# A macaron layer on one core: the first norm spread between the decode's picks, and the first feed-forward in a ring of three PSUM banks

## The reference

```python
x = x + 0.5 * ffn(layernorm(x))      # w = lut[idx]; silu(x Wg) * (x Wu), then Wd; inner size 688
x = x + mamba2(layernorm(x))         # 64 heads of 64, state 128, one group, chunk scan, gated RMS norm
x = x + 0.5 * ffn(layernorm(x))
```

## Time and profile before

| | |
|---|---|
| median of 3 runs | 1440.45 us (1440.12 to 1440.48) |
| profiled execution, device time | 1438.42 us |
| its span, first to last instruction | 1436.7 us |
| mean granted TensorE clock | 0.977 of full |
| PE busy | 1320.8 us, 92% of the span |
| DVE, ACT, POOL busy | 1184.9, 1001.2 and 846.8 us |

### The profile page before, as it was taken

One profiled execution on the slowest core, in us unless ns is written; L12 is line 12 of the kernel. 1 busy time (PEld: TensorE's weight loads), 2 busy tenths in 40 slices (PEclk: granted clock), 3 DMA queues, 4 the chain that ended last, 5 costly groups with the idle time before them and its releaser, 6 DMA issues.

```text
span 1436.7 us, 26981 instructions
## 1 busy us (share of the span) xinstructions
PE 1320.8 (92%) x8896; PEld 1127.6 (78%) x8896; DVE 1184.9 (82%) x2643; ACT 1001.2 (70%) x2043; POOL 846.8 (59%) x920
## 2 busy tenths in 40 slices
PE   5889886757999999999999999999999999998998
PEld 4788775645888888888888888888888888876887
DVE  5862534575999999999999999999999999997542
ACT  1114434566889888878988888898888889883432
POOL 1005211004678787977878787787878778765322
PEclk9999998988999999999999999999999999998999
DMA  6221000223454355444365454444545534345000
GB/s 131 67 89 37 16 1 15 67 60 78 113 123 106 97 126 119 119 121 114 102 112 129 112 123 119 107 105 123 123 114 119 115 100 119 110 109 201 16 16 30
DMA packets 102090, 136.49 MB, mean 95 GB/s; under 512 B 27744, under 2 KB 49856, under 8 KB 101824
## 3 DMA queue, kind: packets, MB, share of 16 engines
q1 hardware_dynamic: 99840, 132.67, 36.7%
q10 hardware_dynamic: 2112, 2.10, 0.4%
HBM read 124.76 MB, written 9.96 MB: 94 GB/s over the span
## 4 chain that ended last, share of the span: by engine, by line
PE 45%; DVE 25%; issue 11%; ACT 3%; DVEq 0%; POOLq 0%; POOL 0%; ACTq 0%
PE psum L38 10%; PE psum L40 9%; PE psum L39 9%; PE psum L1667 6%; DVE xs L1219 5%; PE psum L1656 4%; DVE inner L1270 4%; PE psum L1644 3%; DVE M L1246 3%; DVE psum L1278 3%; DVE xend L1236 3%; DVE mixed L1300 2%; PE psum L1633 2%; DVE carry L1270 1%; DVE xdt L1229 1%
## 5 line engine op out<-in xcount | busy, mean ns | idle before, releaser
L797 ACT ACTIVATE M<-cum_row,cum_table 128x128 f32<-128x128 f32 x1024 | 312.0, 390 | 0.0
L1219 DVE SCALAR_TENSOR_TENSOR xs<-psum,conv_w_sb,xs 128x509 f32<-128x509 f32 (+2 forms) x384 | 282.9, 737 | 0.4
L958 POOL TENSOR_TENSOR hid_lo<-hid,hid_hi 128x512 fp32r<-128x512 f32 x128 | 206.9, 1616 | 71.4 <-PE psum L40 65.4
L1004 POOL TENSOR_TENSOR hid<-hid,sg 128x512 f32<-128x512 f32 x128 | 165.7, 1294 | 91.8 <-DVE hid L1287 91.7
L990 POOL TENSOR_TENSOR squares<-squares,sq 128x512 f32<-128x512 f32 x124 | 160.2, 1292 | 66.6 <-ACT sq L774 66.6
L1246 DVE TENSOR_TENSOR M<-M,CB 128x1024 f32<-128x1024 f32 x128 | 184.5, 1442 | 0.0
L1667 PE MATMUL psum<-M,xdt 128*64 128x128 f32 x2048 | 140.8, 279 | 18.8 <-DVE psum L1278 18.7
L1667 PEld LDWEIGHTS psum<-M,xdt 128*64 128x64 f32 x2048 | 110.7, 137 | 41.4 <-DVE M L1246 22.9
L779 ACT ACTIVATE sg<-psum 128x512 f32<-128x512 f32 x128 | 75.1, 587 | 96.8 <-PE psum L40 89.2
L811 ACT ACTIVATE xs<-psum,conv_b_sb,conv_w_sb 128x512 f32<-128x512 f32 x128 | 99.1, 775 | 60.8 <-PE psum L40 60.1
L1644 PE MATMUL psum<-xend,B_tok 128*128 128x128 f32 x1024 | 138.7, 279 | 2.0 <-DVE carry L1270 1.1
(11 more groups left out here) (197 smaller groups left out, 3420.2 us busy)
## 6 DMA issues: line engine op xcount, KB each, us to landing
cum_row<-cum_scratch SPq DMA_DIRECT2D x256, 256.0 KB, 4.4
e_row<-e_scratch SPq DMA_DIRECT2D x256, 128.0 KB, 3.3
xw_raw<-L_attn_in_proj_w_dram SPq DMA_DIRECT2D x32, 128.0 KB, 4.8
wo_raw<-L_attn_out_proj_w_dram SPq DMA_DIRECT2D x32, 128.0 KB, 4.5
gw_raw<-L_attn_in_proj_w_dram SPq DMA_DIRECT2D x16, 256.0 KB, 5.6
x_res<-_attn_hidden_states_dram ACTq DMA_DIRECT2D x4, 512.0 KB, 9.2
x_scratch<-x_res SPq DMA_DIRECT2D x4, 512.0 KB, 2.6
x_res<-x_scratch SPq DMA_DIRECT2D x1, 2048.0 KB, 9.2
```

The costliest lines, as they stand in the source:

```text
L797: last = nc.scalar.activation(M[:, v % 3, h, c * CH:(c + 1) * CH], cum_row[:, v % 2, h, c * CH:(c + 1) * CH], ACT.Relu, bias=scalar_of(CUM ...
L958: nc.gpsimd.tensor_tensor(hid_lo[:], hid[:, v % 2, :], hid_hi[:, v % 2, :].bitcast(F32), ALU.subtract).then_inc(hid_lo_done, 1)
L1004: nc.gpsimd.tensor_tensor(hid[:, v % 2, :], hid[:, v % 2, :], sg[:, v % 8, :], ALU.mult).then_inc(hid_done, 1)
L1219: nc.vector.scalar_tensor_tensor(xs[:, v % 7, shift:], psum[:, X_BANK + v % 2, 0:TT - shift], tap_of(v, step), xs[:, v % 7, shift:], ALU.m ...
```

## The change

**Decode.** The statistics of `ln1` are taken one row of tokens behind a pick, from (0,3) to (1,2); variance behind (1,3), reciprocal root behind (1,5), and only tile 0 is normalised, row by row, behind (1,6) to (1,9). PE turns only tile 0 there, behind (1,11); tiles 1 to 3 are normalised behind ticks 0, 2 and 4 and turned in ticks 1, 3 and 5. `weights_lo` is cut in three pieces of 512 columns behind picks. The banks of the decode are swapped: gate 3 to 5, up 0 to 2, down 3 to 5; PE's first tick waits for the low parts of gate and up alone, and the first `ffn_down` for that of down. SP now issues gate's indices first, then the table, then the loads of x (ACT issues none), then up's.

**First FFN.** Gate and up share a ring of three banks: gate of tick k uses bank 2k%3 and waits for the multiplication of tick k-2, up uses (2k+1)%3 and waits for silu of tick k-1. Bank 3 goes to dt and the cumulative sums. ACT makes the high part of tick k in tick k, not in k+1. Each hand-written list is split in a part ahead of and a part behind a tick's main instruction, and each consumer of a chain stands a tick or half a tick behind its producer. dt is projected tile by tile. The last ticks' work and slots -8 to -6 are written out in `fill`; the low part of B and C of tile 2 is prepared within the ticks, that of tile 3 and dt of tiles 2 and 3 in slots -6 to 0.

The diff, cut to its core:

```diff
-    dec_bank = {"gate": 0, "up": 3, "down": 0}
+    dec_bank = {"gate": 3, "up": 0, "down": 3}
     FFN_TICKS = NT * MT
+    DT_BANKS, Z_BANK = (3, 3, 2, 4), 3
+    CUM_BANKS, TOTAL_BANKS, ROW_BANKS = (3, 7), (3, 6), ((3, 2), (6, 7))
+    gate_bank = lambda k: 2 * k % 3
+    up_bank = lambda k: (2 * k + 1) % 3
...
+            load_idx("gate", gate_idx)
+            sp.dma_start(lut_sb[:], lut.partition_broadcast(P)).then_inc(lut_in, 16)
+            for g in range(NT):
+                sp.dma_start(x_res[:, g * CPT:(g + 1) * CPT, :],
+                             x_rows[:, g * CPT:(g + 1) * CPT, :]).then_inc(x_in[g], 16)
+            load_idx("up", up_idx)
...
+            def before_hi(k):
+                for T in range(NT - 1):
+                    if k == MT * (T + 1) + 2:
+                        ln2.scalar_sqrt(act, T + 1, T * CPT, (T + 1) * CPT)
+                    if k == MT * (T + 1) + 3:
+                        ln2.scalar_hi(act, T)
+                if k == 11:
+                    silu_bc(0)
+                if k == 17:
+                    silu_bc(1)
+                if k == 18:
+                    dt_ln(0)
+
...
+                if k == 10:
+                    evac_bc(0, (6, 7))
                 if k == 11:
-                    evac_bc(0, (6, 7))
-                if k == 13:
-                    silu_bc(0)
-                if k == 14:
                     evac_B_tok(0, 6)
+                if k == 12:
+                    evac_dt(0)
+                if k == 16:
+                    evac_dt(1)
+                    evac_bc(1, (6, 7))
                 if k == 17:
-                    evac_dt(0)
-                if k == 18:
-                    evac_bc(1, (6, 7))
-                if k == 19:
+                    evac_B_tok(1, 6)
                     dt_exp(0)
-                if k == 20:
-                    dt_ln(0)
-                    silu_bc(1)
                 if k == 21:
-                    evac_B_tok(1, 6)
+                    decays(0)
+                if k == 22:
+                    evac_bc(2, (6, 7))
                 if k == 23:
-                    decays(0)
-                if k == 24:
+                    silu_bc(2)
+                    rows(0)
+                    evac_B_tok(2, 6)
...
             for k in range(FFN_TICKS):
-                if k >= 1:
-                    ffn_hi(k - 1)
                 ffn_silu(k)
-                prep(k)
-            ffn_hi(FFN_TICKS - 1)
+                if k in (1, 3, 5):
+                    ln1.scalar_hi(act, (k + 1) // 2)
+                before_hi(k)
+                ffn_hi(k)
+                after_hi(k)
...
+            def before_mult(k):
+                if k == 18:
+                    dt_plus_one(0)
+                if k == 19:
+                    dt_sum(0)
+                if k == 20:
+                    copy_cum(0)
+                if k == 21:
+                    to_end_arg(0)
+                if k == 23:
+                    taps_bc(2, 1, 7)
+
...
+                        ffn_add(T)
+                        stats2(T)
                     if k == b + 2:
-                        stats2(T)
+                        normalise2(T)
                     if k == b + 3:
-                        normalise2(T)
-                    if k == b + 4:
                         ln2.vector_lo(dve, T)
+                if k == 10:
+                    taps_bc(0, 0, 6)
+                    taps_bc(0, 1, 7)
...
-                    if i == 0 and k in (3, 5, 7, 9):
-                        stats1((k - 3) // 2)
-                    if (i, k) == (0, 9):
+                    if i == 0 and k >= 3:
+                        stats1(k - 3)
+                    if i == 1 and k < 3:
+                        stats1(k + 13)
+                    if (i, k) == (1, 3):
                         ln1.vector_variance(dve, 0, NC)
-                    if (i, k) == (0, 11):
+                    if (i, k) == (1, 5):
                         ln1.vector_rstd(dve, 1, 0, NC)
-                        ln1.vector_normalise(dve, 0)
...
+                    if i == 1 and 6 <= k < 6 + CPT:
+                        ln1.normalise_of(k - 6)
+                    if i == 1 and 10 <= k < 13:
+                        weights_lo(0, k - 10)
+                    if i == 1 and 13 <= k < 13 + KT:
+                        ln1.lo_of(dve, 0, k - 13)
+                    if i == 2 and k in (2, 4, 6):
+                        weights_lo(1, k // 2 - 1)
+            for third in range(3):
+                weights_lo(2, third)
             for k in range(FFN_TICKS):
-                if k % MT == 2 and k > MT:
-                    ffn_add(k // MT - 1)
+                before_mult(k)
                 ffn_mult(k)
-                prep(k)
+                if k in (0, 2, 4):
+                    ln1.vector_normalise(dve, k // 2 + 1)
+                if k in (1, 3, 5):
+                    ln1.vector_lo(dve, (k + 1) // 2)
+                after_mult(k)
...
-                for what, b, done, free in (("gate", k % 2, gate_done, silu_done), ("up", 2 + k % 2, up_done, h_done)):
-                    if k >= 2:
-                        pe.wait_ge(free, k - 1)
+                for what, b, done in (("gate", gate_bank(k), gate_done), ("up", up_bank(k), up_done)):
+                    if what == "gate" and k >= 2:
+                        pe.wait_ge(h_done, k - 1)
+                    if what == "up" and k >= 1:
+                        pe.wait_ge(silu_done, k)
...
             def ffn_down(k):
                 T, m = divmod(k, MT)
                 pe.wait_ge(f_lo_done, k + 1)
+                if k == 0:
+                    pe.wait_ge(w_lo_done, 9)
...
+            def before_down(k):
                 if k == 9:
                     ln2.tensor_turn(pe, 0)
                 if k == 10:
                     proj_bc(0, (6, 7))
-                if k == 13:
-                    pe.wait_ge(bc_done, 2)
-                    turn_B(0, 6)
-                    make_CB(0, 7)
+                if k == 12:
+                    proj_dt(0)
                 if k == 15:
...
                 if k == 16:
-                    proj_dt(0)
+                    pe.wait_ge(zT_done, 1)
+                    proj_dt(1)
+                    proj_bc(1, (6, 7))
                 if k == 17:
-                    pe.wait_ge(zT_done, 2)
-                    proj_bc(1, (6, 7))
-                if k == 18:
-                    pe.wait_ge(bc_done, 3)
                     turn_z(0)
...
                 if k == 22:
-                    pe.wait_ge(ln2.lo_done, KT * 3)
-                    cums(0)
+                    proj_bc(2, (6, 7))
+
+            def after_down(k):
+                if k == 11:
+                    turn_B(0, 6)
+                    make_CB(0, 7)
+                if k == 17:
+                    turn_B(1, 6)
+                    make_CB(1, 7)
+                if k == 19:
+                    cum_sums(0)
+                if k == 20:
+                    totals(0)
                 if k == 23:
+                    pe.wait_ge(h_done, FFN_TICKS)
                     turn_cum(0)
...
+            def fill(s):
+                if s == -8:
+                    turn_B(2, 6)
+                    make_CB(2, 7)
+                    proj_x(0)
+                    pe.wait_ge(x_done, NT)
+                    proj_g(0)
+                if s == -7:
+                    proj_x(1)
+                    pe.wait_ge(B_tok_done, 3)
+                    pe.wait_ge(CB_done, 3)
+                    ln2.tensor_turn(pe, NT - 1)
+                    proj_g(1)
+                if s == -6:
                     pe.wait_ge(cumT_done, 2 * BATCH)
...
                     decode(i, k)
-                    if (i, k) == (0, 13):
-                        turn1(0)
-                    if (i, k) == (1, 1):
-                        turn1(1)
-                    if (i, k) == (1, 5):
-                        turn1(2)
-                    if (i, k) == (1, 9):
-                        turn1(3)
+                    if (i, k) == (1, 11):
+                        ln1.tensor_turn(pe, 0)
             for k in range(FFN_TICKS):
                 ffn_in(k)
+                if k in (1, 3, 5):
+                    turn1((k + 1) // 2)
+                before_down(k)
                 if k >= 2:
                     ffn_down(k - 2)
-                prep(k)
+                after_down(k)
             ffn_down(FFN_TICKS - 2)
+            ffn_down(FFN_TICKS - 1)
...
+                if s == -1:
+                    pe.wait_ge(B_tok_done, NT)
+                    pe.wait_ge(CB_done, NT)
+                    cum_sums(1)
+                    totals(1)
+                if s == 0:
+                    turn_cum(1)
...
```

More of the change, by code:

```diff
@@ L634, in ffn_silu @@
                     act.wait_ge(h_done, k - 1)
[L635 removed]
+                nc.scalar.activation(f_sg[:, k % 2, :], bank(gate_bank(k)), ACT.Silu).then_inc(silu_done, 1)
             def split_x_hi(p):
@@ L678, in evac_B_tok, with evac_dt @@
```

(38 more changed lines are left out.)

261 lines of the change are left out of this document (105 added, 156 removed).

## The result

The changed kernel takes 1379.8 us (median of 4, 1379.49 to 1380.41) against 1440.47 us: ratio 0.9574, 95% interval 0.9559 to 0.9589. The forecast was 1371.5 us, with a range of 1361 to 1393. The total of the profiled execution fell by 58.6 us.

| stretch | before | forecast | after |
|---|---|---|---|
| to the first pick | 11.99 | 6.0 | 6.35 |
| to the first FFN matmul | 89.9 | 70.5 | **89.30** |
| to the gate of tick 8 | 34.2 | 35.3 | 35.63 |
| to the end of the last down product | 119.07 | 94.9 | 92.26 |
| to item 8 | 78.35 | 65.4 | 61.91 |

The account below looks back on a forecast made before the run. Before the loop's steady groups, PE was taken to wait on consumers ordered too close behind their producers. Terms -6.0 - 19.4 + 1.1 - 24.2 - 12.9 - 7.5 = -68.9 us gave a median of 1371.5 us, range 1361 to 1393.

Parts of the forecast that it names:

- Start, -6.0: Up to the first pick: gate's indices loaded first let it start at 6.0 us, not 11.99; bounds 0 and -8.
- Decode, -19.4: First pick to first FFN matmul: 70.5 us instead of 89.9, with small DVE pieces between picks and the 3.33 us gap gone.
- likeliest case: Whole kernel: the summed terms hold, median 1371.5 us, own range 1364 to 1380, chance 0.60.
- Ticks 0 to 8, +1.1: First FFN matmul to gate of tick 8: removing the gap gives -1.8 us, three added turns cost +3.0.
- Ticks 8 to 23, -24.2: Tick 8 to the end of the last down product: 94.9 us instead of 119.07; bounds -27 and -10.
- 2.7 us of waits I followed: Ticks 8 to 23: remaining PE waits, at the turns of 9 and 15 and the turn of the sums in tick 23.
- for what I don't see: Ticks 8 to 23: an allowance of 3 us for unseen stalls, added to PE's work and the followed waits.
- The ring: First FFN, rival: up's wait for the previous tick's silu makes ticks as long as the chain; 1450 at 7.5 us, chance 0.02.
- Loop's start, -12.9: Last down product to item 8: 65.4 us instead of 78.35, ACT the limit from item 3; bounds -16 and 0.
- Slots 0 to 4, -7.5: Loop's first slots: rows first removes out_proj's wait, from 39.36 us toward a steady group's 31.6; bounds -8 and 0.
- Neither the ticks nor the loop's start were held elsewhere: Two rivals: the ticks still stall, giving -12, 1384 us (0.17); the loop's start is bound elsewhere, 1392 us (0.12).
- better than forecast: Whole kernel, rival: no unseen stalls and -8 at the start, 1362 us, chance 0.05.

Follow-up runs that it names:

- e3: The kernel before with only the new order of loads (gate's indices, table, x from SP, up's indices): 1440.08 us, ratio 1.0005.
- e1: The changed kernel with D split in DRAM and loaded in rows of 128 bytes, not 4-byte packets: 1360.38 us, ratio to before 0.9440.
- e11: e1 with the sixteen statistics of the first norm in fours again, behind picks 3, 5, 7 and 9 of gate: 1360.94 us.
- e5: e1 with the decode of before put back (statistics, low parts, transposes, banks, first tick's wait), new order of loads kept: 1376.8 us.
- e10: e1 with silu of B and C behind the high part and PE's turn of B half a tick earlier, ticks 11 and 17: 1365.3 us.
- e7: The kernel before with only the ring of three banks for gate and up and its two waits: 1440.1 us, ratio 0.9995.
- e8: e1 with ACT's high part of tick k, and what stands behind it, put back to tick k+1 ahead of silu: 1361.08 us.
- e6: e1 with ACT's rows of the second half put back to the end of slot 0: 1367.2 us.
- e2: The changed kernel with the two loads of d_sb moved behind the first X, output and gate weights in SP's queue: 1381.49 us, single run.
- e9: e1 with the taps of C of tile 2 behind the last multiplication, not ahead of it: 1356.52 us, ratio to before 0.9421.

## Why the prediction was right, and where its sum was not

**Start, -6.0.** -5.6. Right in size, though the last load to land was the table and not gate's indices, but on its own worthless as long as the fetch stood at 65 us (e3), which my sum did not see: it added stretches as if each passed its gain on.

**Decode, -19.4.** This step failed: -0.6. The sentence "From the first pick to the first FFN matmul: 1.2 + 7.5 + 44 x 1.336 (58.8) + 1.0 + 2.0 = 70.5 us" has no term for PE's own instructions coming late: it assumes that they are always there. With them there it is right: e1 has 76.25 - 6.69 = 69.6 us. What took its place is one stop of 16.6 us. The clock fell to its lower level (1.2 GHz) during it and was back only at 71.4 us; half of the 3.6 us from the end of the stop is my estimate of what that cost, 1.8 us. So the first FFN matmul, which was to be at 75 to 78 us, came at 95.65. No rival of mine had this. That the time lies in the likeliest case's own range (1364 to 1380), by 0.2 us, is luck: 18.8 us lost here, some 9 won below. Without the stop it would have come out just under the whole range (e1, 1360.4). My reason for single statistics (1.40 us in one place stops PE) was weaker than I took it for (e11). By e5 the decode's gain is real; I have not split it among the gap for down, the transposes and the rest.

**Ticks 0 to 8, +1.1.** +1.4. A tick with a turn takes 5.10 us, one without 4.22, read on ACT's silus:

```profile
113.52 0.60 ACT L653 ACTIVATE ffn_silu_gate<-psum 128x512 f32<-128x512 f32 x1 [0.91 <-PE psum L40]
117.74 0.60 ACT L653 ACTIVATE ffn_silu_gate<-psum 128x512 f32<-128x512 f32 x1 [0.89 <-PE psum L40]
122.84 0.60 ACT L653 ACTIVATE ffn_silu_gate<-psum 128x512 f32<-128x512 f32 x1 [0.38 <-PE psum L40]
```

**Ticks 8 to 23, -24.2.** -26.8. PE's own work, 89.2 by hand, is 90.23 busy, with 3.4 us of it at the lower clock. Of the 2.7 us of waits I followed, only that of tick 23 is there, and of the 3 "for what I don't see" nothing. PE's only wait in the stretch:

```profile
PE psum L1583 <- DVE ffn_hidden L1102: 2.0, 1, 2.0
```

The cause, distance to the producer, is shown by e10 for B and C of two tiles, 4.9 us of the 26.8. For the rest of the chain (dt, the sums, the residual) it is argued: the waits of the earlier trace rows are gone, and no run moves those pieces back one by one. The ring (e7) and the earlier high part (e8) have no share of their own in the gain.

**Loop's start, -12.9.** -16.4. From the last down product to item 3 20.2 us (I had 19), on to item 8 41.7 (44 with 6 of waits). The 2.4 us for a slower clock were too many, it is 0.97. PE's waits are small and spread:

```profile
PE psum L1684 <- DVE carry L1309: 2.0, 2, 1.3
PE psum L1568 <- DVE ez L1174: 1.7, 1, 1.7
PE psum L38 <- issue: 1.6, 2, 0.9
```

**Slots 0 to 4, -7.5.** -10.5 in this stretch. I took a steady group, 31.6, as the floor, but these slots need 28.9, since part of PE's work for them is already done when ACT reaches item 8: 185 matmuls are left, where a steady group has 217. The mechanism, rows ahead, is shown, with a net of 7.5 us over this stretch and the one ahead (e6).

**The rivals.** The ring does not bind: e7, and in the changed kernel PE waits for no silu in ticks 8 to 23. Neither the ticks nor the loop's start were held elsewhere. The 1362 of "better than forecast" does not follow from what it names: 3 us of unseen stalls and 2 at the start give 1366.5.

## What to carry to other kernels

A break of 0.3 us with nothing behind it but "issue" can be the visible end of a deadline: look at what lands just before it, and ask what happens when the engine gets there sooner. Before speeding up a start, list the DMA's tiny packets: here 16 KB in 4096 packets occupied 39 us and were hidden only because PE was slow. When a consumer waits in an in-order queue, half a tick of other work in front of it can be the whole cure (e10).

## What was unexpected of the hardware

**Tiny packets are not equal.** Between 20 and 26 us the DMA moved 8149 packets of 4 bytes (those of the tables by channel, `conv_w_sb`, `conv_b_sb` and `norm_sb`, among them), 1358 per us; those of `d_sb`, which read D again for each partition, went at 106 per us, a thirteenth of that rate. The queue view for 20 to 26 us:

```profile
q1 hardware_dynamic: 8149, 0.03, 76.9%
```

The Trainium skill, "DMA: Bandwidth & Descriptors", "Why small descriptors are slow (HBM only)", has a fixed cost per packet. That alone would make the two rates alike. The packets of `d_sb` took 4.7% of the engines' time, so that the engines mostly stood idle between them; why they came so slowly is open. Open is also what exactly a block of instructions waits for: in the kernel before one block still passed at 33 us, when the slow packets had begun, and the next came at 65.

**A wait of 2 us sometimes costs 3.5.** At tick 23 PE waits 2.0 us. In the profile of the changed kernel the clock is then at its lower level for 3.4 us. Three of its microseconds:

```profile
217.00:218.00 1.00, 0.00 (x0) 0.00 (x0) 1.00 (x2) 0.00 (x0) 0.00 (x0) 1.00 0.00 0
219.00:220.00 1.00, 1.00 (x7) 0.85 (x6) 0.00 (x0) 1.00 (x3) 1.00 (x1) 0.50 0.00 0
222.00:223.00 1.00, 1.00 (x11) 1.00 (x10) 0.00 (x0) 1.00 (x3) 0.00 (x0) 1.00 0.00 0
```

In the profiles of e1, e6 and e8, with the same wait, it stays at 1.00. From silu of tick 23 to the evacuation of item 0's gate the changed kernel, e2, e5, e10 and e11 take 15.9 us, and e1, e6 and e8 14.4; e9, without the wait, takes 12.4. That fits e9's gain of 3.9 in the median, where the wait alone would give 2.0; that the clock is the rest was read from the profiles and not tested by itself.
